# Sums of squares of the queries on ACT, and the turned probabilities widened later in each slot

## The chip, the cores and the metric

One core of one Trainium2 chip runs the kernel. The metric is the device time of one execution in microseconds, the median of several.

## What is computed

The input x is 64 sequences of 128 tokens of width 512, with a context of the same shape. The layer is cross attention (16 query heads and 4 key/value heads of width 128), followed by a mixture of 12 experts with 2 chosen per token. Cut to the part that matters here:

```python
q = (layernorm(x) @ Wq).reshape(B, S, 16, 128)
k = (ctx @ Wk).reshape(B, S, 4, 128)
v = (ctx @ Wv).reshape(B, S, 4, 128)
q = rms_norm(q, q_norm_w)            # q * rsqrt(mean(q*q over the head) + eps) * w
k = rms_norm(k, k_norm_w)
probs = softmax(q @ k.T / sqrt(128))
x = x + (probs @ v) @ Wo
x = x + ffn(layernorm(x))            # top 2 of 12 experts, with a capacity
```

## The kernel before, in words

The attention stage is one loop over 64 batches of 128 tokens. Each batch b has four slots g = 0..3, one for each key/value head with its four query heads; u = 4b + g numbers them. All engines walk through the same slots, each with a hand-written order of operations in a function `body`, and they are tied by semaphores alone. Products in full precision are made as three products of high and low parts, so nearly every tensor is split by ACT (the high part, a rounded copy) and DVE (or POOL for x and the context, the low part, a difference). The parts of the queries, of the keys and of the probabilities are written in 16 bits and turned by a DMA transpose that SP issues.

In a slot PE does `scores` of the slot's heads (L760), half of the next batch's `keys` or `values`, the `queries` of three slots ahead (L716), `route` (g=2) or `positions` (g=3, L806) of the experts' gate, `out_project` of two slots back (L788) and `attend` of one slot back (L776). `queries` use two PSUM banks in turn and wait for `q_lo`, DVE's signal that the bank is read out. `attend` and the gate's products share one bank, which is free after `ot_lo`, DVE's half of `split_o`.

The softmax of a slot goes back and forth: DVE takes the `maxima` (L1032 and L1035), ACT the exponentials with their row sums in `exps` (L891, one instruction per head, each followed by a read of the accumulator), DVE the reciprocals and the product in `normalise` (L1041, L1044), ACT and DVE split the result in `split_p` (L899, L1050), SP turns it in `turn_p` (L630), and one slot later ACT and DVE widen the turned halves to 32 bits in `widen_p` (L905, L1057).

The norm of the queries (three slots ahead): ACT squares the bank of 512 columns into another PSUM bank in `square_q` (L874), DVE sums each head in `sum_q` (L1017), POOL adds the epsilon and takes the power -1/2 in `rms_q` (L1289, L1292), and ACT and DVE scale and split the queries two slots ahead in `split_q` (L881, L1023). The sums of squares lie in `q_ssq`, 4 columns; the semaphore `q_ss` says that they are there and `q_m` that POOL has read them.

ACT's order in a slot: `split_o` (two slots back), `widen_p` (one back), then in g=0 `split_xn2` (L916), in g=1 `split_v` (L855), in g=3 `split_k` (L866), then `exps`, `square_q`, in g=0 `split_x` (L850) and in g=3 `split_c` (L845) for coming batches, `split_p`, `split_q`. DVE's order: in g=2 `residual`, then `maxima`, `split_o` (L971), `widen_p`, the halves of `split_xn2`, `split_v` or `split_k`, `norm2` (g=3), `normalise`, small work for the gate, `sum_q`, `split_p`, `split_q`, and at the end of g=0 `stats_x` and `place`, of g=1 `sum_k`, of g=2 `norm_k`, `choose` and `stats_2`. POOL's order: `split_x` (g=0) or `split_c` (g=3), `rms_q`, and in g=1 the `scatter` of table entries (L1304) and `rms_k`. After the loop the experts are computed in a second stage, which the change does not touch.

The helper that gives the slot k further on is

```python
def off(b, g, k):
    return b + (g + k) // NG, (g + k) % NG
```

Of the kernel before, what the change touches and what calls it, by code (L numbers as in the profile page):

```python
# [11 lines left out]
HPG = NH // NG  # L12
# [16 lines left out]
QS, KS, PS = 16.0, 64.0, 16384.0  # L29
# [370 lines left out]
def build(nc, x, xT, cT, wq, wk, wv, wo, qw, kw, gateT, w13, w2T, out):  # L400
    f32, f32r, bf16, f16, i32, u32 = (mybir.dt.float32, mybir.dt.float32r, mybir.dt.bfloat16,
                                      mybir.dt.float16, mybir.dt.int32, mybir.dt.uint32)
    ACT = mybir.ActivationFunctionType
    AX = mybir.AxisListType
# [5 lines left out]
    def wait(eng, sem, n, apart=False):  # L410

        if isinstance(n, int) and n <= 0:
            return
        if apart:
            wait_apart(eng, (sem, n))
        else:
            eng.wait_ge(sem, n)
# [17 lines left out]
    def live(b):  # L435
        return not isinstance(b, int) or 0 <= b < NB

    def off(b, g, k):

        return b + (g + k) // NG, (g + k) % NG  # L440

    keep = ExitStack()
    with keep:
        def sem(name):
            return keep.enter_context(nc.semaphore(name))
# [11 lines left out]
        with ExitStack() as ctx:  # L457
# [41 lines left out]
            q_ssq, q_ms, q_rms = sm(4), sm(4), [sm(4), sm(4)]  # L499
# [15 lines left out]
            Q_BS, K_B, V_B, S_B, OT_B, WO_B, SQ_B = pb[0:2], pb[2], pb[3], pb[4], pb[5], pb[6], pb[7]  # L515

            def heads(bank):
                return bank[:, :].rearrange("p (h t) -> p h t", h=HPG)
# [14 lines left out]
            k_sqd, k_ss, k_m, k_r, k_nrm, k_hi, k_lo = (sem(n) for n in (  # L533
                "k_squared", "k_sumsq", "k_meansq", "k_rms", "k_normed", "k_hi", "k_lo"))
            v_hi, v_lo = sem("v_hi"), sem("v_lo")
            q_sqd, q_ss, q_m, q_r, q_hi, q_lo = (sem(n) for n in (
                "q_squared", "q_sumsq", "q_meansq", "q_rms", "q_hi", "q_lo"))
            sc_done, mx_done, nm_done, exp_done, rs_done, p_nrm, p_hi, p_lo = (sem(n) for n in (
                "scores_done", "max_done", "negmax_done", "exp_done", "rsum_done", "probs_done", "p_hi", "p_lo"))
            pt_hi, pt_lo, ot_done, ot_hi, ot_lo = (sem(n) for n in ("pt_hi", "pt_lo", "ot_done", "ot_hi", "ot_lo"))  # L540
# [298 lines left out]
            def _(act):  # L839
# [28 lines left out]
                def square_q(b, g):  # L868
                    u = 4 * b + g
                    wait(act, q_done, u + 1)  # L870
                    wait(act, q_ss, u)
                    if g == 1:
                        wait(act, k_ss, b + 1)
                    nc.scalar.activation(SQ_B[:, :], Q_BS[g % 2][:, :], ACT.Square, scale=1.0 / QS).then_inc(q_sqd, 1)  # L874

                def split_q(b, g):
                    u = 4 * b + g
# [7 lines left out]
                def exps(b, g):  # L885
                    u = 4 * b + g
                    wait(act, nm_done, u + 1)
                    wait(act, p_lo, u)
                    for h in range(HPG):
                        cols = slice(h * 128, (h + 1) * 128)  # L890
                        ex = nc.scalar.activation(probs[:, cols], S_B[:, cols], ACT.Exp, bias=nmax[:, h:h + 1],  # L891
                                                  scale=esc, accum_out=psums[:, h:h + 1])
                    ex.then_inc(exp_done, 1)
# [7 lines left out]
                def widen_p(b, g):  # L901
                    u = 4 * b + g
                    wait(act, d_pT, 16 * (u + 1))
                    wait(act, ot_done, u)
                    nc.scalar.copy(ptp[0][:, :, :], pT16[:, HI, :]).then_inc(pt_hi, 1)  # L905
# [27 lines left out]
                def body(b):  # L933
                    for g in range(NG):
                        cur, near, far = (b, g), off(b, g, 2), off(b, g, 3)
                        before, last = off(b, g, -1), off(b, g, -2)
                        if live(last[0]):
                            split_o(*last)
                        if live(before[0]):
                            widen_p(*before)  # L940
                        if g == 0 and live(b - 2):
                            split_xn2(b - 2)
                        if g == 1 and live(b):
                            split_v(b)
                        if g == 3 and live(b + 1):
                            split_k(b + 1)
                        if live(b):
                            exps(*cur)
                        if live(far[0]):
                            square_q(*far)  # L950
                        if g == 0 and live(b + 1):
                            split_x(b + 1)
                        if g == 3 and live(b + 2):
                            split_c(b + 2)
                        if live(b):
                            split_p(*cur)
                        if live(near[0]):
                            split_q(*near)
                        if g == 1 and live(b + 1):
                            square_k(b + 1)  # L960
                        if g == 3 and live(b - 2):
                            exp_diff(b - 2)

                loop(act, body)


            @block.vector
            def _(dve):
# [38 lines left out]
                def split_v(b):  # L1007
# [1 line left out]
                    nc.vector.scalar_tensor_tensor(out=vp[1][:, :, :], in0=V_B[:, :].rearrange("p (g t) -> p g t", g=NG),  # L1009
                                                   scalar=1.0 / PS, in1=vp[0][:, :, :].bitcast(f32),  # L1010
                                                   op0=ALU.mult, op1=ALU.subtract).then_inc(v_lo, 1)

                def sum_q(b, g):
                    u = 4 * b + g
                    wait(dve, q_sqd, u + 1)
                    wait(dve, q_m, u)
                    nc.vector.tensor_reduce(q_ssq, heads(SQ_B), AX.X, ALU.add).then_inc(q_ss, 1)  # L1017

                def split_q(b, g):
                    u = 4 * b + g  # L1020
# [16 lines left out]
                def normalise(b, g):  # L1037
                    u = 4 * b + g
                    wait(dve, exp_done, u + 1)
                    wait(dve, p_nrm, u)  # L1040
                    nc.vector.reciprocal(rsums, psums).then_inc(rs_done, 1)  # L1041
                    wait(dve, rs_done, u + 1)
                    pv = probs.rearrange("p (h t) -> p h t", h=HPG)
                    nc.vector.scalar_tensor_tensor(out=pv, in0=pv, scalar=PS,  # L1044
                                                   in1=rsums[:, :, None].broadcast_to([128, HPG, 128]),
                                                   op0=ALU.mult, op1=ALU.mult).then_inc(p_nrm, 1)
# [6 lines left out]
                def widen_p(b, g):  # L1053
                    u = 4 * b + g
                    wait(dve, d_pT, 16 * (u + 1))
                    wait(dve, ot_done, u)
                    nc.vector.tensor_copy(ptp[1][:, :, :], pT16[:, LO, :]).then_inc(pt_lo, 1)  # L1057
# [117 lines left out]
                for l in range(NLOT):  # L1175
                    if l + 1 < NLOT and LOTS[l + 1][0] == "q":
                        n, part = LOTS[l + 1][1], stage(l + 1)
# [12 lines left out]

                def body(b):
                    for g in range(NG):
                        cur, near, far = (b, g), off(b, g, 2), off(b, g, 3)
                        before, last = off(b, g, -1), off(b, g, -2)
                        if g == 2 and live(b - 1):
                            residual(b - 1)
                        if live(b):
                            maxima(*cur)
                        if live(last[0]):
                            split_o(*last)  # L1200
                        if live(before[0]):
                            widen_p(*before)
                        if g == 0 and live(b - 2):
                            split_xn2(b - 2)
                        if g == 1 and live(b):
                            split_v(b)
                        if g == 3 and live(b + 1):
                            split_k(b + 1)
                        if g == 3 and live(b - 1):
                            norm2(b - 1)  # L1210
                        if live(b):
                            normalise(*cur)
                        if g == 2 and live(b - 2):
                            copy_logits(b - 2)
                        if g == 3 and live(b - 2):
                            count(b - 2)
                        if live(far[0]):
                            sum_q(*far)
                        if live(b):
                            split_p(*cur)  # L1220
                        if live(near[0]):
                            split_q(*near)
                        if g == 0 and live(b + 1):
                            stats_x(b + 1)
                        if g == 0 and live(b - 3):
                            place(b - 3)
                        if g == 1 and live(b + 1):
                            sum_k(b + 1)
                        if g == 2 and live(b + 1):
                            norm_k(b + 1)  # L1230
                        if g == 2 and live(b - 2):
                            choose(b - 2)
                        if g == 2 and live(b - 1):
                            stats_2(b - 1)

                loop(dve, body)


# [133 lines left out]
```

## Time and profile before

| | us |
|---|---|
| median of 3 runs (lowest, highest) | 2702.43 (2699.23, 2703.63) |
| the profiled execution | 2700.49 |
| its span | 2698.8 |
| PE busy (matmuls) | 2445.5, 91% |
| weight loads | 1883.8, 70% |
| DVE busy | 2081.5, 77% |
| ACT busy | 1646.8, 61% |
| POOL busy | 1106.9, 41% |
| mean granted TensorE clock | 0.958 |

The span runs from the first to the last instruction; a run's time is a little longer. Some 90 us at the start load and split the weights, the batches of attention follow until about 2350 us, and the experts come last. Busy shares are means over these stages. Matmuls are pipelined, so that one of 512 columns is shown as 0.39 us while they start 0.23 us apart.

### The profile page before, as it was taken

The page shows a single profiled execution, that of the slowest core. Times are in us where ns is not written, and L with a number is a line of the kernel's source. Part 1 is how long each engine was busy: PE and PEld are TensorE (multiplying, and loading weights), DVE is VectorE, ACT ScalarE, POOL GpSimd, SP SyncE. Part 2 cuts the span into 40 slices and gives each one's busy share as a digit, 9 for nine tenths or more (in the row PEclk, how much of TensorE's full clock was granted, in tenths as well). Part 3 has the DMA queues.
Part 4 walks back from the last instruction along what each step waited for, and adds up shares of the span by engine and source line. Part 5 has one row for each costly group of instructions (what it writes and reads, how often), then busy time and mean ns, then how long its engine had stood idle before and what let it go on. Part 6 is the DMA issues. An engine that isn't in the chain of part 4 may idle for free. (4 is left out here: it accounts for less than half of the span.)

```text
span 2698.8 us, 51748 instructions
## 1 busy us (share of the span) xinstructions
PE 2445.5 (91%) x12985; PEld 1883.8 (70%) x12985; DVE 2081.5 (77%) x5478; ACT 1646.8 (61%) x4789; POOL 1106.9 (41%) x1279
## 2 busy tenths in 40 slices
PE   3899999999999999999999999999999999739983
PEld 3677777777777777777777777777777777525541
DVE  5678888888888888888888888888888888626652
ACT  4566666666666666666666666666666666515541
POOL 0334334333333443433333334344333333248885
PEclk8999999999999999999999999999999999968775
DMA  7455555555555555555555555555555555439997
GB/s 210 85 114 115 120 122 117 117 123 118 123 117 118 113 116 124 117 118 119 121 121 119 119 112 115 123 120 118 117 124 117 124 113 111 89 107 182 183 176 96
DMA packets 778098, 331.20 MB, mean 123 GB/s; under 512 B 695340, under 2 KB 707884, under 8 KB 778032
## 3 DMA queue, kind: packets, MB, share of 16 engines
q1 hardware_dynamic: 754960, 287.61, 47.9%
q0 software_dynamic: 22912, 43.16, 8.9%
q8 instruction: 13, 0.21, 0.0%
q14 instruction: 21, 0.17, 0.0%
q10 hardware_dynamic: 192, 0.04, 0.0%
HBM read 108.15 MB, written 57.71 MB: 61 GB/s over the span
## 5 line engine op out<-in xcount | busy, mean ns | idle before, releaser
L905 ACT CAST pt_hi<-work 128x512 fp32r<-128x512 f16 x256 | 159.0, 621 | 652.6 <-DMA work<-work 652.6
L891 ACT ACTIVATE work<-pb,small 128x128 f32<-128x128 f32 x1024 | 454.0, 454 | 47.2 <-DVE small L1035 47.0
L788 PE MATMUL pb<-wo_hi,ot_hi 128*128 128x512 f32 x1024 | 418.8, 409 | 34.9 <-DVE ot_lo L971 34.8
L716 PE MATMUL pb<-wq_hi,x_hi 128*128 128x512 f32 x1024 | 400.9, 391 | 29.7 <-POOL x_lo L1266 22.5
L788 PE MATMUL pb<-wo_hi,ot_lo 128*128 128x512 f32 x1024 | 400.7, 391 | 0.0
L788 PE MATMUL pb<-wo_lo,ot_hi 128*128 128x512 f32 x1024 | 400.4, 391 | 0.0
L716 PE MATMUL pb<-wq_lo,x_hi 128*128 128x512 f32 x1024 | 400.0, 391 | 0.0
L716 PE MATMUL pb<-wq_hi,x_lo 128*128 128x512 f32 x1024 | 399.6, 390 | 0.0
L1289 POOL TENSOR_TENSOR small<-small 128x4 f32<-128x4 f32 x256 | 170.7, 667 | 500.3 <-DVE small L1017 500.3
L1023 DVE SCALAR_TENSOR_TENSOR work<-pb,small,work 128x128 f16<-128x128 f32 x1024 | 286.9, 341 | 47.1 <-ACT work L881 47.1
L881 ACT ACTIVATE work<-pb,small 128x128 f16<-128x128 f32 x1024 | 290.5, 365 | 0.5 <-DMA work<-work 0.4
L1292 POOL TENSOR_TENSOR small<-small 128x4 f32<-128x4 f32 x256 | 258.4, 1009 | 29.5 <-POOL small L1289 18.7
L1050 DVE TENSOR_TENSOR work<-work 128x512 f16<-128x512 f32 x256 | 250.2, 977 | 17.6 <-ACT work L899 11.6
L788 PEld LDWEIGHTS pb<-wo_hi,ot_hi 128*128 128x128 f32 x1024 | 192.6, 188 | 95.6 <-DVE ot_lo L971 61.7
L1266 POOL TENSOR_TENSOR x_lo<-work,x_hi 128x512 fp32r<-128x512 f32 x64 | 82.6, 1291 | 425.9 <-ACT x_hi L850 379.5
L716 PEld LDWEIGHTS pb<-wq_hi,x_hi 128*128 128x128 f32 x1024 | 192.7, 188 | 80.4 <-issue 28.5
L760 PEld LDWEIGHTS pb<-work 128*128 128x128 f16 x3072 | 172.8, 98 | 99.9 <-issue 57.1
L760 PE MATMUL pb<-work 128*128 128x128 f16 x3072 | 216.5, 220 | 22.7 <-DMA work<-work 21.3
L716 PE MATMUL pb<-wkv_hi,c_hi 128*128 128x512 f32 x512 | 223.0, 435 | 0.0
L788 PEld LDWEIGHTS pb<-wo_hi,ot_lo 128*128 128x128 f32 x1024 | 192.9, 188 | 42.4
L716 PEld LDWEIGHTS pb<-wq_hi,x_lo 128*128 128x128 f32 x1024 | 192.8, 188 | 40.9
L716 PEld LDWEIGHTS pb<-wq_lo,x_hi 128*128 128x128 f32 x1024 | 192.8, 188 | 39.1
(144 smaller groups left out, 5307.0 us busy)
## 6 DMA issues: line engine op xcount, KB each, us to landing
work<-x SPq DMA_DIRECT2D x128, 256.0 KB, 3.4
work<-cT SPq DMA_DIRECT2D x64, 256.0 KB, 2.7
work<-xT SPq DMA_DIRECT2D x64, 256.0 KB, 3.1
out<-work SPq DMA_DIRECT2D x64, 256.0 KB, 4.1
xn_scratch<-work SPq DMA_DIRECT2D x64, 256.0 KB, 2.2
work<-work SPq DMA_TRANSPOSE x640, 3.0
work<-wq SPq DMA_DIRECT2D x16, 256.0 KB, 3.4
work<-wo SPq DMA_DIRECT2D x16, 256.0 KB, 3.6
```

Of the source, the lines that this page charges most:

```text
L716: mm = nc.tensor.matmul(bank[:, :], lhs[a][:, c, :], rhs[b_][:, c, :], start=(c == 0 and n == 0), stop=(c == NC - 1 and n == 2))
L760: mm = nc.tensor.matmul(S_B[:, h * 128:(h + 1) * 128], qT16[:, 4 * a + h, :], kT16[:, 4 * b_ + g, :], start=(n == 0), stop=(n == 2))
L788: mm = nc.tensor.matmul(WO_B[:, :], otp[a][:, h, :], wop[b_][:, g * HPG + h, :], start=(g == 0 and h == 0 and n == 0), stop=(g == NG - 1 a ...
L881: hi = nc.scalar.activation(q16[:, h, :], Q_BS[g % 2][:, h * 128:(h + 1) * 128], ACT.Copy, scale=q_rms[g % 2][:, h:h + 1])
L891: ex = nc.scalar.activation(probs[:, cols], S_B[:, cols], ACT.Exp, bias=nmax[:, h:h + 1], scale=esc, accum_out=psums[:, h:h + 1])
L905: nc.scalar.copy(ptp[0][:, :, :], pT16[:, HI, :]).then_inc(pt_hi, 1)
L1023: lo = nc.vector.scalar_tensor_tensor(out=q16[:, 4 + h, :], in0=Q_BS[g % 2][:, h * 128:(h + 1) * 128], scalar=q_rms[g % 2][:, h:h + 1], in ...
L1050: nc.vector.tensor_tensor(p16[:, LO, :], probs.rearrange("p (h t) -> p h t", h=HPG), p16[:, HI, :], ALU.subtract).then_inc(p_lo, 1)
L1266: nc.gpsimd.tensor_tensor(xp[1][:, :, :], raw_x.rearrange(by_chunk, c=NC), xp[0][:, :, :].bitcast(f32), ALU.subtract).then_inc(x_lo, 1)
L1289: nc.gpsimd.tensor_tensor(q_ms, q_ssq, eps_x.broadcast_to([128, HPG]), ALU.add).then_inc(q_m, 1)
L1292: nc.gpsimd.tensor_tensor(q_rms[g % 2], q_ms, neghalf, ALU.pow).then_inc(q_r, 1)
```

## The change

It squares the queries on ACT one head at a time, with the row sum taken by the same instruction (`accum_out`) and written to `q_ssq`; DVE's `sum_q` and the semaphore `q_squared` between the two are gone. And it moves `widen_p` on ACT from before to behind `exps`, and on DVE from before to behind `normalise`.

```diff
@@ square_q, ACT
                 def square_q(b, g):
                     u = 4 * b + g
                     wait(act, q_done, u + 1)
-                    wait(act, q_ss, u)
+                    wait(act, q_m, u)
                     if g == 1:
                         wait(act, k_ss, b + 1)
-                    nc.scalar.activation(SQ_B[:, :], Q_BS[g % 2][:, :], ACT.Square, scale=1.0 / QS).then_inc(q_sqd, 1)
+                    for h in range(HPG):
+                        cols = slice(h * 128, (h + 1) * 128)
+                        sq = nc.scalar.activation(SQ_B[:, cols], Q_BS[g % 2][:, cols], ACT.Square, scale=1.0 / QS,
+                                                  accum_out=q_ssq[:, h:h + 1])
+                    sq.then_inc(q_ss, 1)
@@ body, ACT
                         if live(last[0]):
                             split_o(*last)
-                        if live(before[0]):
-                            widen_p(*before)
                         if g == 0 and live(b - 2):
                             split_xn2(b - 2)
...
                         if live(b):
                             exps(*cur)
+                        if live(before[0]):
+                            widen_p(*before)
                         if live(far[0]):
                             square_q(*far)
@@ DVE
-                def sum_q(b, g):
-                    u = 4 * b + g
-                    wait(dve, q_sqd, u + 1)
-                    wait(dve, q_m, u)
-                    nc.vector.tensor_reduce(q_ssq, heads(SQ_B), AX.X, ALU.add).then_inc(q_ss, 1)
-
@@ body, DVE
                         if live(last[0]):
                             split_o(*last)
-                        if live(before[0]):
-                            widen_p(*before)
                         if g == 0 and live(b - 2):
                             split_xn2(b - 2)
...
                         if live(b):
                             normalise(*cur)
+                        if live(before[0]):
+                            widen_p(*before)
                         if g == 2 and live(b - 2):
                             copy_logits(b - 2)
                         if g == 3 and live(b - 2):
                             count(b - 2)
-                        if live(far[0]):
-                            sum_q(*far)
                         if live(b):
                             split_p(*cur)
```

## Rows read from the trace of the kernel before

**Rows 1.** Windows: us; busy us of PE, PEld, DVE, ACT, POOL; clock, DMA share, GB/s.

```profile
1000.00:1600.00 600.00, 577.93 (x3219) 456.58 (x3218) 496.57 (x1386) 395.51 (x1197) 232.87 (x289) 1.00 0.54 119
2320.00:2337.00 17.00, 10.94 (x66) 8.54 (x65) 12.21 (x38) 10.22 (x33) 3.63 (x4) 0.90 0.52 108
```

**Rows 2.** Timeline of PE: start us, us, engine, line, operation, count, idle before.

```profile
1210.76 0.19 PE L806 MATMUL pb<-small,tri 128*128 128x24 bf16 x1 [0.86 <-DVE ot_lo L971]
...
1214.79 0.84 PE L760 MATMUL pb<-work 128*128 128x128 f16 x12 [0.32 <-DMA work<-work]
...
1216.92 0.39 PE L716 MATMUL pb<-wq_hi,x_hi 128*128 128x512 f32 x1
...
1219.64 0.39 PE L788 MATMUL pb<-wo_hi,ot_hi 128*128 128x512 f32 x1
...
1228.55 0.50 PE L788 MATMUL pb<-wo_hi,ot_hi 128*128 128x512 f32 x1 [0.50 <-DVE ot_lo L971]
...
1246.18 0.19 PE L806 MATMUL pb<-small,tri 128*128 128x24 bf16 x1 [0.46 <-DVE ot_lo L971]
```

**Rows 3.** Waits of the whole span: us in total, times, longest us.

```profile
ACT pt_hi L905 <- DMA work<-work: 652.6, 256, 4.5
...
DVE small L1041 <- ACT work L891: 202.1, 194, 2.0
...
DVE work L1023 <- ACT work L881: 47.1, 131, 0.9
```

**Rows 4.** Timeline of ACT in slot g=2.

```profile
1236.24 0.46 ACT L891 ACTIVATE work<-pb,small 128x128 f32<-128x128 f32 x1
...
1237.99 0.60 ACT L874 ACTIVATE pb<-pb 128x512 f32<-128x512 f32 x1
1239.08 0.62 ACT L899 CAST work<-work 128x512 f16<-128x512 f32 x1 [0.48 <-DVE work L1044]
1239.61 1.14 ACT L881 ACTIVATE work<-pb,small 128x128 f16<-128x128 f32 x4
```

**Rows 5.** Timeline of DVE in slot g=2 and the start of g=3.

```profile
1235.71 0.50 DVE L1035 TENSOR_SCALAR small<-small 128x4 f32<-128x4 f32 x1
...
1239.07 0.68 DVE L1017 TENSOR_REDUCE small<-pb 128x4 f32<-128x512 f32 x1
1239.73 0.69 DVE L1050 TENSOR_TENSOR work<-work 128x512 f16<-128x512 f32 x1
...
1244.58 0.69 DVE L1032 TENSOR_REDUCE small<-pb 128x4 f32<-128x512 f32 x1
1245.30 0.23 DVE L1035 TENSOR_SCALAR small<-small 128x4 f32<-128x4 f32 x1
```

**Rows 6.** Timeline of DVE, second step of the maxima in g=0 and g=1.

```profile
1216.62 0.23 DVE L1035 TENSOR_SCALAR small<-small 128x4 f32<-128x4 f32 x1
...
1227.67 0.23 DVE L1035 TENSOR_SCALAR small<-small 128x4 f32<-128x4 f32 x1
```

**Rows 7.** Timeline of ACT in slot g=0.

```profile
1218.09 0.62 ACT L905 CAST pt_hi<-work 128x512 fp32r<-128x512 f16 x1 [2.88 <-DMA work<-work]
1218.62 0.61 ACT L916 CAST work<-work 128x512 f16<-128x512 f32 x1
1219.14 0.45 ACT L891 ACTIVATE work<-pb,small 128x128 f32<-128x128 f32 x1
...
1222.04 0.62 ACT L899 CAST work<-work 128x512 f16<-128x512 f32 x1
```

**Rows 8.** Timeline of ACT, first exponential of g=1, then exponential and `split_p` of g=3.

```profile
1228.22 0.45 ACT L891 ACTIVATE work<-pb,small 128x128 f32<-128x128 f32 x1
...
1245.57 0.46 ACT L891 ACTIVATE work<-pb,small 128x128 f32<-128x128 f32 x1 [0.73 <-DVE small L1035]
...
1248.41 0.62 ACT L899 CAST work<-work 128x512 f16<-128x512 f32 x1
```

**Rows 9.** Timeline of POOL, second scatter of the batch.

```profile
1235.22 0.99 POOL L1304 DMA_INDIRECT token_table<-small  x1 [0.30 <-issue]
```

**Rows 10.** Timeline of SP, issue of the turn of the probabilities.

```profile
1215.02 1.24 SPq L630 DMA_TRANSPOSE work<-work  x1
```

More of the change, by code:

```diff
@@ L535, in build @@
             v_hi, v_lo = sem("v_hi"), sem("v_lo")
-            q_sqd, q_ss, q_m, q_r, q_hi, q_lo = (sem(n) for n in (
-                "q_squared", "q_sumsq", "q_meansq", "q_rms", "q_hi", "q_lo"))
+            q_ss, q_m, q_r, q_hi, q_lo = (sem(n) for n in (
+                "q_sumsq", "q_meansq", "q_rms", "q_hi", "q_lo"))
             sc_done, mx_done, nm_done, exp_done, rs_done, p_nrm, p_hi, p_lo = (sem(n) for n in (
@@ L1192, in body @@
                     for g in range(NG):
-                        cur, near, far = (b, g), off(b, g, 2), off(b, g, 3)
+                        cur, near = (b, g), off(b, g, 2)
                         before, last = off(b, g, -1), off(b, g, -2)
```

## The prediction

> **What bounds the kernel now.** I read the windows first, since the page's shares mix stages. In the 600 us in the middle PE is busy for 96%, DVE for 83% and ACT for 66%, with the granted clock at 1.00 [rows 1]. A busy PE could mean that only its own work counts, so I looked for its gaps in its timeline [rows 2]. One batch (four slots) takes 1246.18 - 1210.76 = 35.42 us, and in it PE stands still three times: for `ot_lo` of DVE before `positions` in slot g=3 (0.86 us, and 0.46 a batch later), for a turned operand before `scores` in g=0 (0.32), for `ot_lo` again before `out_project` in g=1 (0.50). Each is about 0.16 us longer than it says, because a matmul's modelled end lies that far behind the time at which the next could have begun. That makes 2.2 us in a period with the 0.86 and 1.8 in one with the 0.46; I take 1.8, and a floor of 33.6 us.
>
> What is PE late for? `ot_lo` comes behind `maxima` on DVE, and `maxima` begins when DVE gets to it, not when the scores are there: the twelve matmuls of g=0 run from 1214.79 for 0.84 us [rows 2], but `maxima` is done only at 1216.62 + 0.23 = 1216.85 [rows 6]. So the next view is the waits [rows 3]: DVE waits for the exponentials 194 times (202 us in all) and for ACT's `split_q` 131 times (47 us), and ACT's largest wait, 653 us for the turned probabilities, stands ahead of the exponentials. Followed in time through slot g=2 [rows 4, 5] this is a closed ring: `maxima` (DVE), exponentials (ACT, four heads from 1236.24 to 1237.99, 1.75 us), `normalise` (DVE), `split_p` (ACT, at 1239.08, after 0.48 us of idling until DVE's product), `split_q` on ACT from 1239.61, `split_q` on DVE, the slot's other DVE work, and the next `maxima` at 1244.58. The other slots look alike. **The ring of ACT and DVE sets the 35.42 us, not PE**, and what counts is what the change adds to it or takes from it. E below is the start of the exponentials.
>
> **The change, part by part.** (1) `sum_q` leaves DVE: 256 reductions of 0.68 us. It lies between `normalise` and DVE's `split_p`, and the latter waits for ACT's `split_p`, which ends at 1239.08 + 0.62 = 1239.70, while `sum_q` runs from 1239.07 to 1239.75 [rows 4, 5]. It is hidden beside ACT's work; without it DVE starts 0.05 us earlier at best, and that meets the wait for `split_q`. I take 0. Its cover is the wait for ACT, and part 3 makes that wait longer.
>
> (2) `widen_p` leaves its place ahead of the exponentials. On ACT in g=0 it sits idle for 2.88 us until the turned probabilities are there, and the exponentials begin at 1219.14 [rows 7] though the maxima were done at 1216.85 [rows 6]. The handover costs 0.04 elsewhere (1245.53 to 1245.57 [rows 5, 8]), so 2.25 us are won. In g=1: 1228.22 against 1227.67 + 0.23 = 1227.90 [rows 6, 8], so 0.28 us. In g=2 and g=3 the exponentials begin 0.03 to 0.04 us after the maxima (1236.21 and 1245.53 [rows 5]): nothing. `split_xn2`, `split_v` and `split_k` stay ahead of them, and their inputs are there long before. On DVE `widen_p` stood in the wait for the exponentials and will stand in the wait for `split_p`: 0.
>
> (3) ACT between the exponentials and `split_p`. Before, the one square (from 1237.99) is hidden beside `normalise`, and `split_p` starts at E + 2.84 in g=2 (1239.08 - 1236.24 [rows 4]), the same in g=3 (1248.41 - 1245.57 [rows 8]) and, by its likeness to g=2, in g=1; E + 2.90 in g=0 (1222.04 - 1219.14 [rows 7]). After, ACT has in a row: exponentials 1.75, `widen_p` 0.53 (1218.09 to the next start at 1218.62 [rows 7]), four squares, in g=0 and g=3 a copy of x or ctx (0.53 again), then `split_p`. No row shows the square of one head with its sum. Two rows bound it. The exponentials have the same form, 128 elements out of PSUM with a sum, and take 1.75 for four [rows 4]. The scaled copies of `split_q`, four without a sum, take 1.14 in all [rows 4], about 1.04 from the first to whatever follows. I take 1.75, the nearer form, and keep 1.04 as the lower end; above 1.75 nothing points, as the square of 512 elements takes 0.60 like a copy. `split_p` then starts at E + 1.75 + 0.53 + 1.75 = E + 4.03 in g=1 and g=2, and E + 4.56 in g=0 and g=3. Added: 1.66 + 1.19 + 1.19 + 1.72 = 5.76 us a batch, all of it in the ring, since what is behind it (`split_p`, `split_q` on ACT, `split_q` on DVE, the next `maxima`) follows without slack. Queued behind the squares on ACT is also `split_o`, which has more than 1 us before DVE asks for it.
>
> (4) POOL's scatter. DVE's second step of `maxima` takes 0.50 us in g=2 against 0.23 in g=3 and ends at 1236.21, together with the scatter, 1235.22 + 0.99 [rows 5, 9]. The sums now come from ACT ahead of `split_p`, so POOL is done with `rms_q` and the scatter earlier against DVE's next `maxima`: 0.27 us won (0 is the other end).
>
> (5) Waits that could be new. The squares need PE's queries of the same slot, which wait for DVE's `split_q` of the slot before. Twelve matmuls take 1219.64 - 1216.92 = 2.72 us [rows 2], with two handovers about 3.0; the ring itself takes 0.91 (`maxima`, less overlap) + 0.04 + 1.75 + 0.53 = 3.2 from there when nothing lies between, as from g=3 to g=0. That is 0.2 us from mattering: 0. The turned probabilities are used 3.07 us after their issue (1215.02 to 1218.09 [rows 7, 10]). By the same count they come 0.5 us before `widen_p` wants them in g=0 and 2 us before in the others: 0. `rms_q` on POOL is wanted a slot later: 0. SP's queue keeps its order; its turns move with the splits that release them, and the queries' turn, issued early in a slot, is wanted in the next.
>
> Sum per batch: 5.76 - 2.25 - 0.28 - 0.27 = **+2.96 us**, a period of 38.4. The last batch has one square left and the first waits for weights, so I count 63 periods: +186 us. The profiled execution took 2700.5 us (span 2698.8), so it becomes 2887; the median of the runs stands 1.9 us higher: 2888. PE then idles 38.4 - 33.6 = 4.8 us a batch, in pieces under 2 us. The clock stood at 1.00 with PE 96% busy and at 0.90 in a stretch where it was 64% busy [rows 1]; here it would be near 88%. Even at 0.90 PE's floor would be 33.6 / 0.9 = 37.3, under 38.4, so I add nothing for it.
>
> **A rule against the rows.** DVE is the busiest engine after PE, and it is relieved of 0.68 us a slot. The Trainium skill, Perfetto Trace Analysis, sections Identifying the Most-Contended Engine and Optimizing Scalar/DVE Operations, says to optimise the engine of highest occupancy, and that offloading to Scalar may make sense if DVE is saturated. By that rule the change is a gain, rival A. The rows do not show DVE saturated: it waits for ACT [rows 3].
>
> **The rivals.** (A) Faster: DVE's queue decides, and its relief counts. For it: 83% busy, and PE's waits end with DVE's `ot_lo`. Then 4 x 0.66 (1239.07 to the next operation [rows 5], at most) and the 2.5 us of part 2 come off, and PE's floor stops it: 63 x 1.8 = 113 us less, 2589. It decides only if ACT still reaches `split_p` by E + 2.84, with squares of at most 2.84 - 1.75 - 0.53 = 0.56 us in all; against it stands the 0.44 of a single exponential. Chance 0.03. (B) The sum is almost free, 1.04 for four squares: 2.96 - 4 x 0.71 = +0.12 a batch, 8 us, 2710. The exponentials' spacing speaks against it. Chance 0.04, over all three outcomes. (C) Slower still: in g=0 the squares wait for the queries (0.2 us of slack) or `widen_p` for its transposes (0.5), or PE's clock falls. Half a microsecond on each wait adds 0.3 us a batch, one and a half adds 1.3: 20 to 80 us, 2910 to 2970. Chance 0.09. That the change doesn't do what it says can be left out: each operation is placed by hand in its engine's order.
>
> **How the numbers follow.** The forecast has 0.84, the rivals 0.03, 0.04 and 0.09. Bounds of its sum: without part 4 and with 64 periods, 3.23 x 64 = 207 us, 2909; with 0.15 us less for a slot's four squares and 62 periods, 2.36 x 62 = 146 us, 2849. With the lower half of C the range is 2848 to 2925. A measurement can tell about 0.2%, 5 us, from nothing: faster 0.04, same 0.01, slower 0.95.
>
> **What the changed profile would show.** A period of 38.4 between the `positions` matmuls. On ACT 1024 squares of some 0.45 us with their sums 0.44 apart, `widen_p` with hardly any idle time before it, the exponentials 0.04 us behind the maxima in every slot, `split_p` at E + 4.0 and E + 4.6 without a wait for DVE. On DVE less work and more waiting for ACT before `split_p`. On PE more idle time before `positions`, and gaps before `queries`, which wait for `q_lo`. I am wrong if four squares take under 1.4 us, if DVE's `split_p` does not wait, or if the exponentials in g=0 still start 2 us late.

## The result, and the profile after

The changed kernel takes 2722.3 us (median of 5 runs, 2715.8 to 2724.3) against 2702.4 us (median of 5, too): a ratio of 1.007, with a 95% interval of 1.0055 to 1.0085. It is slower, as forecast, but by 20 us and not by 186, and the time lies far outside the range.

From the page of the changed kernel, the busy times, and the groups of the exponentials (L895), of DVE's `split_p` (L1048) and of the squares (L876):

```profile
PE 2468.4 (91%) x12985; PEld 1865.9 (69%) x12985; DVE 1934.6 (71%) x5222; ACT 1781.3 (65%) x6581; POOL 1032.1 (38%) x1279
...
L895 ACT ACTIVATE work<-pb,small 128x128 f32<-128x128 f32 x1024 | 455.7, 455 | 541.8 <-DVE small L1033 541.8
L1048 DVE TENSOR_TENSOR work<-work 128x512 f16<-128x512 f32 x256 | 259.7, 1015 | 280.2 <-ACT work L903 280.2
...
L876 ACT ACTIVATE pb<-pb 128x128 f32<-128x128 f32 x1024 | 280.4, 274 | 19.5 <-PE pb L716 19.4
```

DVE is relieved by 147 us and ACT carries 135 us more. DVE's `split_p` (L1048) now waits 280 us for ACT, 1.1 us in every slot; before it waited 12, as the waits of the kernel before have it:

```profile
DVE work L1050 <- ACT work L899: 11.6, 63, 0.7
```

And the instruction that squares one head takes 274 ns, against 455 ns for the exponential of one head.

The waits of the changed kernel that answer to [rows 3]:

```profile
ACT work L895 <- DVE small L1033: 541.8, 256, 3.3
...
DVE work L1048 <- ACT work L903: 280.2, 256, 2.2
...
DVE small L1039 <- ACT work L895: 204.1, 256, 1.9
...
PEld pb L806 <- DVE ot_lo L975: 80.0, 59, 1.7
PE pb L806 <- DVE ot_lo L975: 58.7, 62, 1.7
...
DVE work L1021 <- ACT work L885: 54.3, 131, 4.8
```

ACT's 653 us of waiting for the turned probabilities are gone. What it waits for ahead of the exponentials is now the maxima, in all 256 slots. The ring of ACT and DVE is closed everywhere, and PE waits at `positions` for the DVE half of `split_o`, longer than before (59 us in all against 35).

The timeline of ACT, from slot g=0 into g=1 (the accumulator reads between the rows are left out), which answers to [rows 7, 8]:

```profile
1230.71 0.46 ACT L895 ACTIVATE work<-pb,small 128x128 f32<-128x128 f32 x1 [1.20 <-DVE small L1033]
...
1232.46 0.62 ACT L909 CAST pt_hi<-work 128x512 fp32r<-128x512 f16 x1
1232.99 0.26 ACT L876 ACTIVATE pb<-pb 128x128 f32<-128x128 f32 x1
...
1233.26 0.28 ACT L876 ACTIVATE pb<-pb 128x128 f32<-128x128 f32 x1
...
1234.11 0.62 ACT L850 CAST x_hi<-work 128x512 fp32r<-128x512 f32 x1
1234.62 0.63 ACT L903 CAST work<-work 128x512 f16<-128x512 f32 x1
...
1240.65 0.46 ACT L895 ACTIVATE work<-pb,small 128x128 f32<-128x128 f32 x1 [3.25 <-DVE small L1033]
...
1242.92 0.28 ACT L876 ACTIVATE pb<-pb 128x128 f32<-128x128 f32 x1
...
1244.05 0.62 ACT L903 CAST work<-work 128x512 f16<-128x512 f32 x1
```

From the first exponential to the copy behind the last one it is 1232.46 - 1230.71 = 1.75 us; `widen_p` takes 0.53; the four squares take 1234.11 - 1232.99 = 1.12. `split_p` starts at E + 3.91 in g=0 and E + 3.40 in g=1, where 4.56 and 4.03 were forecast.

The timeline of PE, the first gate matmul of two batches, which answers to [rows 2]:

```profile
1223.47 0.19 PE L806 MATMUL pb<-small,tri 128*128 128x24 bf16 x1 [0.94 <-DVE ot_lo L975]
...
1259.45 0.19 PE L806 MATMUL pb<-small,tri 128*128 128x24 bf16 x1 [0.90 <-DVE ot_lo L975]
```

The period is 1259.45 - 1223.47 = 35.98 us (36.01 as a mean over 49 periods), against 35.45 as a mean of the same periods before: +0.56 us.

Where the 22 us of the span come from is seen in first and last starts, `scores` on PE (L760) and the experts' gathers on POOL (L173). Before:

```profile
L760 PE MATMUL pb<-work x3072: 216/219/314, 80.4 to 2339.1; 128*128 128x128 f16 x192
...
L173 POOL DMA_INDIRECT xg<-xn_scratch,from x84: 992/998/1534, 2388.8 to 2620.7; - x84
```

After:

```profile
L760 PE MATMUL pb<-work x3072: 216/219/330, 80.5 to 2368.9; 128*128 128x128 f16 x192
...
L173 POOL DMA_INDIRECT xg<-xn_scratch,from x84: 997/1002/1438, 2415.6 to 2642.5; - x84
```

The stretch of the scores grew by 29.7 us, from 2258.7 to 2288.4. From there to the first gather it is 49.7 us before and 46.7 after, 3.0 less, and from the first gather to the end 310.0 and 305.1 (the spans are 2698.8 and 2720.7), 4.9 less. The last is not the change's doing: nothing of it reaches the experts, and in the eleven other profiled runs of this document the same stretch takes 296 to 300 us, whatever was edited in the loop. Why it was 310 and 305 us in the first two traces is open. Without these 4.9 us the difference of the spans would be 27 us.

### The profile page after: what moved, and what is told of

It is laid out like the page before. It is cut to its first block and busy times, and to the rows that moved or that the text cites. A ratio compares the mean times of both kernels' runs of the same rounds, so it can differ in the third digit from the quotient of the medians.

```text
span 2720.7 us, 53029 instructions
## 1 busy us (share of the span) xinstructions
PE 2468.4 (91%) x12985; PEld 1865.9 (69%) x12985; DVE 1934.6 (71%) x5222; ACT 1781.3 (65%) x6581; POOL 1032.1 (38%) x1279
## 5 line engine op out<-in xcount | busy, mean ns | idle before, releaser
L895 ACT ACTIVATE work<-pb,small 128x128 f32<-128x128 f32 x1024 | 455.7, 455 | 541.8 <-DVE small L1033 541.8
L1048 DVE TENSOR_TENSOR work<-work 128x512 f16<-128x512 f32 x256 | 259.7, 1015 | 280.2 <-ACT work L903 280.2
L716 PE MATMUL pb<-wq_hi,x_hi 128*128 128x512 f32 x1024 | 411.1, 401 | 27.5 <-POOL x_lo L1262 22.3
L1285 POOL TENSOR_TENSOR small<-small 128x4 f32<-128x4 f32 x256 | 107.6, 420 | 533.9 <-ACT pb L876 533.9
L876 ACT ACTIVATE pb<-pb 128x128 f32<-128x128 f32 x1024 | 280.4, 274 | 19.5 <-PE pb L716 19.4
L1288 POOL TENSOR_TENSOR small<-small 128x4 f32<-128x4 f32 x256 | 258.4, 1010 | 29.5 <-POOL small L1285 18.7
L716 PEld LDWEIGHTS pb<-wq_hi,x_hi 128*128 128x128 f32 x1024 | 192.6, 188 | 101.0 <-DVE work L1021 36.3
L760 PEld LDWEIGHTS pb<-work 128*128 128x128 f16 x3072 | 172.8, 98 | 79.3 <-issue 54.1
L760 PE MATMUL pb<-work 128*128 128x128 f16 x3072 | 216.6, 220 | 3.1 <-DMA work<-work 3.0
```

Of the source, the lines that this page charges most:

```text
L716: mm = nc.tensor.matmul(bank[:, :], lhs[a][:, c, :], rhs[b_][:, c, :], start=(c == 0 and n == 0), stop=(c == NC - 1 and n == 2))
L760: mm = nc.tensor.matmul(S_B[:, h * 128:(h + 1) * 128], qT16[:, 4 * a + h, :], kT16[:, 4 * b_ + g, :], start=(n == 0), stop=(n == 2))
L876: sq = nc.scalar.activation(SQ_B[:, cols], Q_BS[g % 2][:, cols], ACT.Square, scale=1.0 / QS, accum_out=q_ssq[:, h:h + 1])
L1048: nc.vector.tensor_tensor(p16[:, LO, :], probs.rearrange("p (h t) -> p h t", h=HPG), p16[:, HI, :], ALU.subtract).then_inc(p_lo, 1)
L1285: nc.gpsimd.tensor_tensor(q_ms, q_ssq, eps_x.broadcast_to([128, HPG]), ALU.add).then_inc(q_m, 1)
L1288: nc.gpsimd.tensor_tensor(q_rms[g % 2], q_ms, neghalf, ALU.pow).then_inc(q_r, 1)
```

## The experiments

The kernel before ran beside each group of runs again. Its medians were 2693.9, 2688.9 and 2692.1 us, so ratios are compared, not times. Theory 1 is the prediction's ring of ACT and DVE. The expectations of the first four kernels name a time on the scale of the first measurement (kernel before at 2702 us), those of the later ones a time on the scale of the runs made by then (kernel before at 2694 or 2689 us). "Period" is the mean distance of two batches in the middle of the loop.

**Only the widening moved** (`w1_widen_only`).

```diff
@@ kernel before, body of ACT
-                        if live(before[0]):
-                            widen_p(*before)
...
                             exps(*cur)
+                        if live(before[0]):
+                            widen_p(*before)
@@ kernel before, body of DVE
-                        if live(before[0]):
-                            widen_p(*before)
...
                             normalise(*cur)
+                        if live(before[0]):
+                            widen_p(*before)
```

> Only widen_p is moved; the one square of 512 on ACT and sum_q on DVE stay. Theory 1 (the ring of ACT and DVE sets the period): the late exponentials of g=0 and g=1 go (2.25 + 0.28 us), split_p starts at E + 1.75 + 0.53 + 0.52 = 2.80, so still E + 2.84 behind normalise in g=1 and g=2, and at E + 3.33 in g=0 and g=3 (+0.42, +0.49). Period 35.45 - 2.53 + 0.91 = 33.8, near PE's floor of 33.6; time about 2600 (2585 to 2625). Theory 2 (the squares, not the order, are what costs; moving widen_p is worth nothing since its transposes are late anyway): 2690 to 2710.

Measured 2577.6 us, ratio 0.9574 (0.9558 to 0.959), which is 2587 us on the scale of the first measurement, at the low end of theory 1; the period is 33.79 us, as forecast. The windows of this kernel (us, then busy us of PE, PEld, DVE, ACT, POOL):

```profile
1000.00:1600.00 600.00, 598.13 (x3373) 478.74 (x3372) 520.11 (x1454) 413.81 (x1260) 236.06 (x302) 1.00 0.56 124
```

PE is busy for 598 of 600 us: the floor is reached. Half of the change is worth 4.3%, and the other half costs more than that.

**Only the squares moved to ACT** (`s1_squares_only`).

```diff
@@ changed kernel, body of ACT
-                        if live(before[0]):
-                            widen_p(*before)
...
                             split_o(*last)
+                        if live(before[0]):
+                            widen_p(*before)
@@ changed kernel, body of DVE: the same, back behind split_o
```

> Only the squares with their sums go to ACT; widen_p stays ahead of the exponentials. Theory 1, with 1.13 us for four squares as the changed kernel's trace has it: split_p at E + 1.75 + 1.13 = 2.88 in g=1 and g=2 (+0.05), E + 3.41 in g=0 and g=3 (+0.50, +0.57), less 0.27 for the scatter; the exponentials of g=0 stay 2.3 us late. Period 36.3, time 2745 to 2765. Theory 2 (relieving DVE of the sum helps): under 2702.

Measured 2782.1 us, ratio 1.034 (1.0322 to 1.0358), slower as theory 1 has it but by 88 us, not by 43 to 63. The period is 36.97 and not 36.3. `split_p` does start where it was expected, at E + 2.88 and E + 3.39. What was missed stands in the timeline of ACT in slot g=2:

```profile
1210.26 0.62 ACT L909 CAST pt_hi<-work 128x512 fp32r<-128x512 f16 x1 [2.18 <-DMA work<-work]
1210.78 0.46 ACT L895 ACTIVATE work<-pb,small 128x128 f32<-128x128 f32 x1
```

Here, too, the exponentials now wait for `widen_p` and that for its transposes, 0.50 us behind the maxima (mean of the middle batches) against 0.05 before. A wait that had just been covered came out when the scatter's 0.27 us went. The rest is 0.13 us in g=0 and 0.05 in g=3, where DVE's `split_p` runs beside POOL's `split_x` and `split_c` and takes longer than before.

The two parts do not add up to the whole: -1.65 and +1.52 us per period make -0.13, and both together give +0.56. The main reason is the 2.84 us from E until DVE's `normalise` is done and `split_p` can start. In g=1 and g=2 either the squares (1.75 + 1.13) or the widening with the old square (1.75 + 0.53 + 0.52) hides in it; both together, 1.75 + 0.53 + 1.13 = 3.41, do not. Summed over the four slots (means of the middle batches), `split_p` starts 0.84 us later behind E with the widening alone, 1.12 us with the squares alone, and 3.20 us with both: 1.24 us more than the two together. Smaller terms work both ways: the scatter's 0.27 us is won in each of the three kernels, and the 0.45 us of new waiting in g=2 is there with the squares alone but not with both.

**The sum kept on DVE** (`a2_sum_kept_on_dve`), by a reduction of the same size, out of SBUF and not PSUM (its semaphore and its spare columns are not shown):

```diff
@@ changed kernel, body of DVE
                             count(b - 2)
+                        if live(b):
+                            wait(dve, p_nrm, 4 * b + g + 1)
+                            wait(dve, again, 4 * b + g)
+                            nc.vector.tensor_reduce(spare, probs.rearrange("p (h t) -> p h t", h=HPG), AX.X,
+                                                    ALU.add).then_inc(again, 1)
```

> The changed kernel with a reduction of 128x512 to 4 columns added on DVE where sum_q stood (it sums the probabilities in SBUF into spare columns that nobody reads, and waits for the product before it, some 0.04 us). Theory 1: it lies in DVE's wait for ACT's split_p and costs nothing, 2715 to 2730 (in g=3, where the count of the gate comes too, it still fits: normalise ends at E + 2.81, widen_p, count and 0.7 make E + 4.1, against split_p's end at E + 4.5). Theory 2 (DVE's work counts): 0.65 us in each of 250 slots, 2722 + 160 = 2880.

Measured 2713.3 us, ratio 1.0073 (1.0056 to 1.009), against 1.007 for the changed kernel; the period is 35.99. The timeline of DVE in slot g=1 of this kernel shows why 256 reductions cost nothing:

```profile
1207.76 0.42 DVE L1056 CAST pt_lo<-work 128x512 fp32r<-128x512 f16 x1
1208.10 0.68 DVE L1219 TENSOR_REDUCE small<-work 128x4 f32<-128x512 f32 x1
1209.09 0.69 DVE L1049 TENSOR_TENSOR work<-work 128x512 f16<-128x512 f32 x1 [0.31 <-ACT work L904]
```

Even behind the added reduction DVE is idle for 0.31 us until ACT's `split_p` is done. The relief of DVE, which the rule on the busiest engine would have counted as a gain, is worth nothing here.

**Where the squares are written** (`a1_squares_to_sbuf`). The remaining question was why a square costs 0.28 us where the exponential costs 0.44.

```diff
@@ changed kernel, square_q of ACT
+            sq_sb = sb("sq_sb", [128, 128])
...
+                        to = (sq_sb[:, :], mean_w[:, :], SQ_B[:, cols], SQ_B[:, cols])[h]
-                        sq = nc.scalar.activation(SQ_B[:, cols], Q_BS[g % 2][:, cols], ACT.Square, scale=1.0 / QS,
+                        sq = nc.scalar.activation(to, Q_BS[g % 2][:, cols], ACT.Square, scale=1.0 / QS,
```

> The changed kernel with the squares of heads 0 and 1 written to SBUF, those of heads 2 and 3 to PSUM as before. Nobody reads the squares themselves, so the result is the same. Theory P (where an instruction with a row sum writes to sets its price: 0.28 us from start to start into PSUM, 0.44 into SBUF as for the exponentials): heads 0 and 1 show about 450 ns, heads 2 and 3 about 275 ns, 0.32 us more per slot, 1.3 per batch, time 2722 + 75 to 85 = about 2800. Theory F (the function or its pointer operands set it): all four 275 ns, 2715 to 2730.

Measured 2705.9 us, ratio 1.0046 (1.0029 to 1.0062). The groups of the squares, heads 2 and 3 (`pb`), head 0 (`sq_sb`) and head 1 (`mean_w`):

```profile
L878 ACT ACTIVATE pb<-pb 128x128 f32<-128x128 f32 x512 | 146.1, 290 | 0.0
...
L878 ACT ACTIVATE sq_sb<-pb 128x128 f32<-128x128 f32 x256 | 73.9, 289 | 21.1 <-PE pb L717 21.1
L878 ACT ACTIVATE mean_w<-pb 128x128 f32<-128x128 f32 x256 | 72.7, 284 | 0.0
```

Theory P falls: all four heads show 284 to 290 ns. From its start to its accumulator read head 1, written to SBUF, is even 37 ns shorter than those written to PSUM (158 against 195), and head 0, the first of the row, 25 ns shorter (170). The period is 0.14 us below the changed kernel's.

**The operands, per head** (`b1_pointers_per_head`).

```diff
@@ changed kernel, square_q of ACT (s_col and b_col: two columns of 128x1 set once, to 1/QS and 0)
+                        more = (dict(scale=1.0 / QS), dict(scale=s_col), dict(scale=1.0 / QS, bias=b_col),
+                                dict(scale=s_col, bias=b_col))[h]
-                        sq = nc.scalar.activation(SQ_B[:, cols], Q_BS[g % 2][:, cols], ACT.Square, scale=1.0 / QS,
-                                                  accum_out=q_ssq[:, h:h + 1])
+                        sq = nc.scalar.activation(SQ_B[:, cols], Q_BS[g % 2][:, cols], ACT.Square,
+                                                  accum_out=q_ssq[:, h:h + 1], **more)
```

> The changed kernel with other operands in the squares: head 0 as before (scale and bias as constants), head 1 its scale read from a column of 128x1, head 2 its bias, head 3 both; the columns hold the same values, so the result is the same. Theory O (each operand read from a column adds to the instruction): the traces so far show 158 ns from an ACTIVATE into SBUF to its accumulator read with constants, 250 to the next copy with one column, 343 with two, so 92 each. Then 195, 288, 288 and 380 ns into PSUM, four squares in 1.50 us instead of 1.13, period 36.0 + 1.5 = 37.5, time 2715 + 90 = about 2805. Theory F (the exponential as a function is what takes longer): all four 195 ns, about 2715.

Measured 2786.4 us, ratio 1.0362 (1.0345 to 1.038), period 37.16. The timeline of ACT over one slot's squares, heads 0 to 3, and the start of `split_p` behind them:

```profile
1205.65 0.28 ACT L879 ACTIVATE pb<-pb 128x128 f32<-128x128 f32 x1
1205.85 0.20 ACT L879 ACTIVATION_READ_ACCUMULATOR pb<-pb 128x1 f32 x1
1205.93 0.34 ACT L879 ACTIVATE pb<-pb,small 128x128 f32<-128x128 f32 x1
1206.18 0.21 ACT L879 ACTIVATION_READ_ACCUMULATOR pb<-pb,small 128x1 f32 x1
1206.28 0.35 ACT L879 ACTIVATE pb<-pb,small 128x128 f32<-128x128 f32 x1
1206.53 0.22 ACT L879 ACTIVATION_READ_ACCUMULATOR pb<-pb,small 128x1 f32 x1
1206.62 0.45 ACT L879 ACTIVATE pb<-pb,small 128x128 f32<-128x128 f32 x1
1206.96 0.22 ACT L879 ACTIVATION_READ_ACCUMULATOR pb<-pb,small 128x1 f32 x1
1207.05 0.64 ACT L906 CAST work<-work 128x512 f16<-128x512 f32 x1
```

The operands set the price. From start to start a head takes 0.28 us with constants, 0.34 with one column (scale or bias alike) and 0.43 with both, which is the exponentials' 0.44. The expected 92 ns per column was right for the second one; the first adds only 54 ns over a square into PSUM with constants, so four come to 1.40 us and not 1.50, and the period is 37.16 us where theory O had 37.5. The time is 97 us above the kernel before, against 111 in theory O (2805 less 2694).

**The function** (`b2_exp_for_square`): the same kernel with `ACT.Exp` in place of `ACT.Square`, so the queries are scaled by other numbers.

> As the kernel with other operands per head, and with the exponential in place of the square, so that the norms of the queries are other numbers. Theory O: the same as with the square, 195, 288, 288 and 380 ns to the accumulator read, time about 2805. Theory F: 190 ns more in every head, whatever its operands, about 2900.

One run, 2785.6 us, period 37.16. The rows of the exponential with constants and with two columns:

```profile
1204.71 0.28 ACT L879 ACTIVATE pb<-pb 128x128 f32<-128x128 f32 x1
...
1205.69 0.44 ACT L879 ACTIVATE pb<-pb,small 128x128 f32<-128x128 f32 x1
```

They are those of the square with the same operands. One run says little of the time, but theory F wanted 190 ns more in every head, and the rows show none; theory F is out.

**All four squares at the predicted price** (`b3_all_heads_pointers`): `scale=s_col, bias=b_col` for every head.

> The changed kernel with the scale and the bias of all four squares read from columns, as the exponentials have them: the price on which the prediction was built. Theory 1 with 0.434 us per square from the last two runs: four in 1.74, split_p at E + 4.0 and E + 4.55, period 36.0 + 4 x 0.61 = 38.4, which was the period predicted; the time is 60 to 62 such periods longer than the changed kernel's, 2713 + 150 = 2855 to 2872 on this chip. If the period is 38.4, every other term of the prediction's sum stands; anything over 0.3 us off would show a term that has been missed.

Measured 2879.2 us, ratio 1.0698 (1.0681 to 1.0714), period 38.57; the time is 7 us above the range expected here. The prediction's 2888 us over 2702.4 is 1.0687, and its period was 38.4. The timeline of ACT has the squares as the prediction had assumed them, four from 1209.32 to 1211.07, 1.75 us, and `split_p` at E + 4.02 (1207.05 to 1211.07):

```profile
1207.05 0.46 ACT L896 ACTIVATE work<-pb,small 128x128 f32<-128x128 f32 x1 [3.38 <-DVE small L1036]
...
1208.81 0.62 ACT L910 CAST pt_hi<-work 128x512 fp32r<-128x512 f16 x1
1209.32 0.44 ACT L877 ACTIVATE pb<-pb,small 128x128 f32<-128x128 f32 x1
...
1211.07 0.64 ACT L904 CAST work<-work 128x512 f16<-128x512 f32 x1
```

**The widening moved on ACT only** (`w2_widen_act_only`): the first half of the first diff.

> The kernel before with widen_p moved on ACT only. Theory 1: the wait that counted was ACT's. DVE's widen_p ahead of normalise has the wait for the exponentials as cover, but in g=0 it may hold split_xn2 and normalise some 0.3 us. Period 33.6 to 33.9, time 2575 to 2590, as with both moved. Theory 2 (both halves are needed): 2600 or more.

Measured 2600.5 us, ratio 0.9674 (0.9658 to 0.969), period 34.17: most of the gain, but 10 us outside what theory 1 was given, and inside what theory 2 was given. DVE in slot g=0:

```profile
1208.89 0.43 DVE L1057 CAST pt_lo<-work 128x512 fp32r<-128x512 f16 x1 [0.65 <-DMA work<-work]
1209.23 0.69 DVE L1084 TENSOR_TENSOR work<-work 128x512 f16<-128x512 f32 x1
1209.83 0.17 DVE L1041 RECIPROCAL small<-small 128x4 f32<-128x4 f32 x1
```

DVE's widening waits for the transposes, `split_xn2` queues behind it, and `normalise` starts back to back, 0.25 us later than the exponentials would allow. So DVE's half of the move is not worth 0, once ACT's is made. The scatter's hold of 0.27 us on `maxima` in g=2 is there in this kernel, too (the second step takes 0.50 us), and not in the kernel with both halves moved. Together that is more than the 0.38 us between the two periods, which fits that PE has almost no idle time left in the other kernel and holds it up a little.

**The squares behind `split_q`** (`a3_squares_last`).

```diff
@@ changed kernel, body of ACT
-                        if live(far[0]):
-                            square_q(*far)
...
                             split_q(*near)
+                        if live(far[0]):
+                            square_q(*far)
                         if g == 1 and live(b + 1):
                             square_k(b + 1)
```

> The changed kernel with its four squares behind split_q on ACT instead of ahead of split_p. Theory 1 (only what stands between the exponentials and split_q counts): split_p starts at E + 2.84 in all slots, in g=0 and g=3 1.75 + 0.53 + 0.53 = 2.81 fits under it, the ring needs 36.0 - 2 x 0.56 - 2 x 1.08 = 32.7, so PE's floor of 33.6 decides: 2562 to 2580, as fast as with widen_p moved alone or a little faster. Theory 2 (ACT's load counts, or the sums that come later hold up rms_q and split_q): above 2620.

Measured 2570.5 us, ratio 0.9559 (0.9539 to 0.958), period 33.76. The windows:

```profile
1000.00:1600.00 600.00, 600.00 (x3379) 480.57 (x3379) 488.98 (x1381) 462.15 (x1766) 210.68 (x303) 1.00 0.56 124
```

ACT is busier than in any other of these kernels (77%), and PE shows no idle time. The same four squares that cost 2.2 us per period ahead of `split_p` (36.01 us against the 33.79 of `w1_widen_only`, which has the old square there) cost nothing behind `split_q`, where PE sets the period.

**The two best, once more and side by side** (`a4_squares_last_again`, `w3_widen_only_again`).

> The changed kernel with the squares last on ACT, once more beside the next kernel on one chip. PE has no idle time left in either, and the periods were 33.76 and 33.80: no difference above 0.3%, 2565 to 2580.

> Only widen_p moved, on both engines, beside the kernel before it in this call: 2570 to 2582.

2573.1 us, ratio 0.9557 (0.9544 to 0.957), and 2575.5 us, ratio 0.9572 (0.9559 to 0.9585). Both beat the kernel before and the changed one by more than 4%; between them nothing can be told.

## Why the prediction was right in sign and wrong in size

- **What bounds the kernel**: right. The ring of ACT and DVE set the period in the kernel before, in the changed one and in the runs at higher prices. Taking work out of the ring brought PE to its floor, 33.76 to 33.79 us, where 33.6 was estimated.
- **Part 1, `sum_q` is worth 0**: right; a reduction of its size put in its place cost nothing (35.99 against 36.01 us).
- **Part 2, 2.25 and 0.28 us won by the late exponentials**: right. They start 0.04 us behind the maxima in all slots, and `widen_p` no longer waits.
- **Part 3, the price of a square with its sum**: this is the step that failed. "I take 1.75, the nearer form" took the exponentials for the same form because shape, source and accumulator agreed. They differ in their operands: `exps` reads scale and bias from columns (`bias=nmax[:, h:h + 1], scale=esc`), `square_q` has constants, and the rows show it in their names, `work<-pb,small` against `pb<-pb`. Measured, four squares take 1.12 to 1.13 us, under the 1.4 that the prediction had named as a sign that it is wrong. The term is then 4 x 0.62 = 2.5 us smaller: 5.76 - 2.5 - 2.80 = +0.48 us a batch instead of +2.96, against a measured +0.56. The lower bound of 1.04 was nearly it, and rival B at 2710 is the case that came closest; it had a chance of 0.04. That the bound came so near is luck: it was built from `split_q`, which reads one column and takes no sum, and the two differences nearly cancel. The range had no room for it: it allowed "0.15 us less for a slot's four squares" although the text's own ends were 0.71 apart.
- The Trainium skill states a price, in ScalarE: Activation LUTs, section What ACT_TABLE_LOAD costs: an ACTIVATE takes 186 ns plus 0.833 ns per element with immediate scale and bias, each pointer operand adds about 93 ns, and neighbours overlap by about 93. By that an estimate for 128 elements is 200 ns before the next start with constants, 293 with one pointer and 386 with two. For the squares of the changed kernel the trace agrees (195 ns to the accumulator read); with columns it shows less, 250 ns with one and 342 to 343 with two. The prediction did not draw on it.
- **Part 4, the scatter**: right in size, 0.27 us. The second step of `maxima` takes 0.23 us in g=2, and the scatter now ends 0.49 us before it begins, as forecast. But the earlier sums are not the only way to win it: in `w1_widen_only`, with the sums still on DVE, the step takes 0.23 us too, although a scatter runs from 0.32 us before its start to 0.66 us behind it. In the kernel before, the scatter began 0.48 us before the step and ended with it. What makes the step wait in one case and not in the other is open.
- **Part 5, no new waits**: right for this change. A term is missing, though. DVE's `split_p` runs beside POOL's split in g=0 and g=3 and takes longer than before, 1.36 us against 1.24 and 1.34 against 1.31 (0.69 in the other slots): from the end of ACT's `split_q` to that of DVE's it is 1.40 us in g=0 against 1.27, and 1.38 in g=3 against 1.34. That adds 0.17 us a batch. On the other side `split_p` starts 3.20 us later in all, and not 5.76 - 2.5 = 3.28. The two together are about the 0.08 us between +0.48 and +0.56. That POOL is what slows `split_p` was not tested.
- **63 periods**: too many by the measure of the trace. 63 x 0.56 would be 35 us, and 29.7 were seen between the first and last scores, because the first three periods are shorter than the later ones (33.7, 34.3 and 35.1 us, where the kernel before has 36.8, 34.6 and 36.8); what bounds them was not followed. The end of the loop gave back 3.0 us, and the experts' 4.9, which do not come from the change, make the measured 20 us smaller still.
- With the one price put right, the prediction's own method gives 63 x 0.48 = 30 us, 2732; with the price left as it was and the kernel made to match it, the measured ratio is 1.0698 where it had 1.0687. The rest of the sum is thereby tested, not only the step that failed. That it fits to 0.1% is in part luck: the period grew by 3.12 us (38.57 against 35.45) and not by 2.96, 0.16 us more for the missing term at `split_p`, which over 63 periods is 10 us, and the first periods and the end of the loop gave about as much back.

## What to carry to other kernels

Before a row is taken as the price of a new instruction, compare all its operands, the scale and bias and where they come from, not only shape, engine and output. Where ACT and DVE hand a tile back and forth, find the ring and ask of each operation whether it stands inside a partner's time that hides it; such cover is used up once, so two edits that are each hidden may not be so together. Work that nobody waits for in this slot belongs behind the last operation that the partner does wait for: the same four squares cost nothing there, where PE sets the period.

## What the runs showed of the hardware

- ACT, 128x128 fp32 from PSUM with a row sum, from the start to the accumulator read: with constants 158 ns into SBUF and 195 ns into PSUM (`a1_squares_to_sbuf`); into PSUM 250 ns with one column as scale or bias and 342 with both (`b1_pointers_per_head`); into SBUF, with both, also 342 (the exponentials). The first of a row takes up to 16 ns more. The accumulator read adds 88 to 93 ns to the spacing.
- Square and exponential take the same time with the same operands: 195, 250, 250 and 342 to 343 ns (`b1_pointers_per_head`, `b2_exp_for_square`).
- DVE's second step of `maxima` (128x4, fp32) took 0.50 us when one of POOL's scatters had begun 0.48 us before it (kernel before), and 0.23 us when one had begun 0.32 us before it and was still running (`w1_widen_only`).
